# A decoder layer on one core: the values become the weight in two column tiles, and VectorE's chain is cut and put in another order

## The reference, cut to what matters

```
q, k, v = x @ Wq, x @ Wkv[:, :1024], x @ Wkv[:, 1024:]     # 16 heads of 64
sim  = q k^T / 8
G    = sigmoid(sim)
P    = min(flip(cumsum(flip(G))), 63)                       # position of key j for query i
E    = q @ pos_emb                                          # 64 table entries for each query
sim += w * E[ceil(P)] + (1 - w) * E[floor(P)]               # w = P - floor(P)
out  = softmax(sim) @ v;  result = concat(out) @ Wout + b_out
```

## Time and profile before

| | us |
|---|---|
| median of 3 runs | 2726.79 (2726.04 to 2726.97) |
| span of the profiled execution | 2722.5 |
| PE busy in the span | 2562.4 (94%) |
| DVE busy | 2256.0 (83%) |
| ACT busy | 1501.2 (55%) |
| POOL busy | 214.1 (8%) |

### The profile page before, as it was taken

One profiled execution on the slowest core, in us unless ns is written; L12 is line 12 of the kernel. 1 busy time (PEld: TensorE's weight loads), 2 busy tenths in 40 slices (PEclk: granted clock), 3 DMA queues, 4 the chain that ended last, 5 costly groups with the idle time before them and its releaser, 6 DMA issues. The chain is left out here.

```text
span 2722.5 us, 69322 instructions
## 1 busy us (share of the span) xinstructions
PE 2562.4 (94%) x18175; PEld 2259.5 (83%) x18175; DVE 2256.0 (83%) x5821; ACT 1501.2 (55%) x2487; POOL 214.1 (8%) x283
## 2 busy tenths in 40 slices
PE   6999999999999999999999999999999997999997
PEld 5888888888888888888888888888888885777776
DVE  6999999999999999999999999999999980222222
ACT  4655565556556555565555655555555552344442
POOL 0000000000000000000000000000000000111111
PEclk9999999999999999999999999999999998999998
DMA  2111111111111111111111111111110102001100
GB/s 81 35 39 35 39 35 39 35 39 35 37 35 37 33 37 33 39 35 39 35 39 35 39 35 39 35 36 37 34 28 25 45 10 74 26 31 35 35 23 8
DMA packets 126696, 97.59 MB, mean 36 GB/s; under 512 B 24078, under 2 KB 124559, under 8 KB 126672
## 3 DMA queue, kind: packets, MB, share of 16 engines
q1 hardware_dynamic: 126672, 97.29, 12.5%
HBM read 13.21 MB, written 2.10 MB: 6 GB/s over the span
## 5 line engine op out<-in xcount | busy, mean ns | idle before, releaser
L494 PE MATMUL out<-V,probsT 128*128 (+1 forms) x8192 | 959.5, 273 | 0.0
L494 PEld LDWEIGHTS out<-V,probsT 128*128 128x128 f32 x8192 | 944.5, 192 | 0.9
L361 ACT ACTIVATE probsT<-ring 128x512 f32<-128x512 f32 x1024 | 584.5, 597 | 503.4 <-PE ring L482 503.4
L482 PEld LDWEIGHTS ring<-ident,probs 128*128 128x128 f32 x4096 | 474.7, 141 | 250.3 <-issue 170.9
L482 PE MATMUL ring<-ident,probs 128*128 128x128 f32 x4096 | 580.1, 274 | 98.4 <-DVE k_lo L704 98.2
L369 ACT ACTIVATE probs<-Sc,nbias 128x1024 f32<-128x1024 f32 x512 | 543.2, 1112 | 232.7 <-DVE nbias L674 232.5
L657 DVE TENSOR_REDUCE mx<-Sc 128x1 f32<-128x1024 f32 (+1 forms) x640 | 636.3, 994 | 0.9 <-PE Sc L474 0.8
L474 PE MATMUL Sc<-k_hi,q_now 128*128 (+1 forms) x1024 | 469.5, 458 | 17.2 <-ACT probs L369 10.3
L621 DVE COPY_PREDICATED z<-mask,z 128x96 f32<-128x96 int16 (+6 forms) x896 | 422.1, 471 | 30.8
L474 PE MATMUL Sc<-k_lo,q_now 128*128 (+1 forms) x1024 | 406.6, 397 | 0.0
L297 POOL TENSOR_TENSOR prod<-frac,z 128x350 f32<-128x350 f32 x128 | 142.5, 1113 | 2085.2 <-DVE z L644 2085.2
(11 more groups left out here) (117 smaller groups left out, 2392.5 us busy)
## 6 DMA issues: line engine op xcount, KB each, us to landing
q_far<-q SPq DMA_DIRECT2D x128, 128.0 KB, 2.0
q_now<-q SPq DMA_DIRECT2D x128, 128.0 KB, 2.0
xv<-xT SPq DMA_DIRECT2D x113, 128.0 KB, 2.2
k_hi<-k_hi SPq DMA_DIRECT2D x128, 64.0 KB, 1.9
k_lo<-k_lo SPq DMA_DIRECT2D x128, 64.0 KB, 1.9
at<-attn SPq DMA_DIRECT2D x16, 512.0 KB, 3.2
q<-stage SPq DMA_DIRECT2D x120, 64.0 KB, 1.9
probs<-in_x_dram SPq DMA_DIRECT2D x4, 512.0 KB, 5.5
```

What stands on the lines that cost most here:

```text
L361: nc.scalar.activation(probsT[:, u, 4 * s:4 * s + 4, :], ring[(k + s) % 2][:, :].rearrange("p (t q) -> p t q", q=P), ACT.Copy).then_inc(sl ...
L482: last = nc.tensor.transpose(ring[(k + s) % 2][:, j * P:(j + 1) * P], probs[:, u, (4 * s + j) * P:(4 * s + j + 1) * P], ident[:, :])
L494: last = nc.tensor.matmul(out[:, 0:VW], probsT[:, u, t, :], V[:, h % 4, t, :], start=t == 0, stop=t == NT - 1)
```

## The change

1. **V as the weight.** V loses its column of ones. At the first g of each head SP copies the head's values into a tile `V_now` (512 KB, `load_values`), once `outputs` of the head before are done. In `outputs` the 64 columns of `V_now[:, t, :]` are now the weight and 128 columns of probsT stream past them. Even t go to partitions 0 to 63 of `out`, odd t to partitions 64 to 127, so there are two column tiles, each with its own sum. ACT copies both halves out (`empty_halves`), and one more matmul against a matrix of two stacked identities (`fold`) adds and transposes them into columns 128 to 191 of `out` (`turn`).
2. **The row sums** come from ACT's exponentials (`accum_out`, one sum for each half). DVE adds the two (`add_halves`) and inverts the sum from SBUF.
3. **DVE's chain** loses mask 7 and the shift by 128. The scans of the next g stand ahead of `last_shift`; `corrections` moves from the end of the body to behind the first `bank_max` of the next body; `scale(g - 1, 0)` moves from the end of body g - 1 to behind `scan_floors` in body g; and `scale(g - 1, 1)` moves behind shift 3. Semaphore `scanned` is split into `scanned` and `shifted`, and three tiles share memory with others (`flo = rnd`, `frac = cut`, `corr = prod`).

```diff
-BITS = 8
+BITS = 7
+TURN = P
...
+            def load_values(g):
+                sp.dma_start(V_now[:, :, :], V[:, (g // PAIRS) % 4, :, :]).then_inc(v_in, 16)
...
+                if head:
+                    wait_apart(sp, out_full, g * 2, waited)
+                    load_values(g)
...
+            def empty_halves(g, u):
+                act.wait_ge(out_full, g * 2 + u + 1)
+                nc.scalar.activation(halves[:, u, :], out[:, 0:P], ACT.Copy).then_inc(halves_out, 1)
...
-                    nc.scalar.activation(probs[:, u, cols], Sc[:, cols], ACT.Exp,
-                                         bias=nbias[:, u:u + 1]).then_inc(exp_done, 1)
+                    nc.scalar.activation(probs[:, u, cols], Sc[:, cols], ACT.Exp, bias=nbias[:, u:u + 1],
+                                         accum_out=sums[:, u, half:half + 1]).then_inc(exp_done, 1)
...
                 exps(g, 0)
+                if not first:
+                    empty_halves(g - 1, 1)
                 if val:
-                    if not first:
-                        act.wait_ge(out_full, g * 2)
                     values(g, base, k)
...
                 if wait_read and tiles[0] == 0:
                     pe.wait_ge(out_read, g * 2 + u)
+                if tiles[0] == 0:
+                    wait_apart(pe, v_in, g // PAIRS * 16 + 16, waited)
                 for t in tiles:
                     if t % 4 == 0:
                         pe.wait_ge(slot_out, base + k + t // 4 + 1)
-                    last = nc.tensor.matmul(out[:, 0:VW], probsT[:, u, t, :], V[:, h % 4, t, :],
-                                            start=t == 0, stop=t == NT - 1)
+                    half = t % 2 * C
+                    last = nc.tensor.matmul(out[half:half + C, 0:P], V_now[:, t, :], probsT[:, u, t, :],
+                                            start=t < 2, stop=t >= NT - 2)
...
+            def turn(g, u):
+                pe.wait_ge(halves_out, g * 2 + u + 1)
+                nc.tensor.matmul(out[:, TURN:TURN + C], halves[:, u, :], fold[:, :],
+                                 start=True, stop=True).then_inc(turned, 1)
...
                     if n < 2:
                         logits(g, 1, n + 2)
+                    if n == 1 and not first:
+                        turn(g - 1, 1)
...
+            def add_halves(g, u):
+                dve.wait_ge(exp_done, g * 4 + u * 2 + 2)
+                nc.vector.tensor_tensor(rowsum[:, u:u + 1], sums[:, u, 0:1], sums[:, u, 1:2],
+                                        ALU.add).then_inc(summed, 1)
...
                 bank_max(g, 0, 0, 0, 1, 2)
+                if not first:
+                    corrections(g)
                 add_window(g, 0)
                 if chain:
                     scan_floors(c)
+                if not first:
+                    scale(g - 1, 0)
                 window_max(g, 0, 1, 2, 4)
...
                 if chain:
-                    shift(c, 7)
+                    shift(c, 6)
                 if proj:
                     k_rest(g + PAIRS, 0)
                 if chain:
-                    shift(c, 6)
-                if chain:
                     shift(c, 5)
-                if not first:
-                    invert(g - 1, 1)
                 bank_max(g, 1, 0, 0, 1, 2)
                 if not first:
-                    scale(g - 1, 1)
+                    add_halves(g - 1, 1)
                 if chain:
                     shift(c, 4)
                 add_window(g, 1)
+                if not first:
+                    invert(g - 1, 1)
                 if chain:
                     shift(c, 3)
+                if not first:
+                    scale(g - 1, 1)
...
                     slopes(c)
-                    last_shift(c)
-                invert(g, 0)
+                add_halves(g, 0)
                 if scan:
                     scan_positions(c + 1)
-                scale(g, 0)
+                invert(g, 0)
                 if scan:
                     round_positions(c + 1)
                 if chain:
-                    corrections(c)
+                    last_shift(c)
```

More of the change, by code:

```diff
@@ L120, in attention @@
         stage = sb("stage", [P, STEP], F32R)
-        V = sb("V", [P, 4, NT, VW])
+        V = sb("V", [P, 4, NT, C])
+        V_now = sb("V_now", [P, NT, C])
+        halves = sb("halves", [P, 2, P])
+        fold = sb("fold", [P, C])
+        sums = sb("sums", [P, 2, 2])
+        rowsum = sb("rowsum", [P, 2])
         q_far = sb("q_far", [P, 2 * P], F32R)
@@ L270, in body @@
                     load_now(g + 1)
-            with sp.Fori(0, LASTV // PAIRS - 1) as h:
-                with sp.Fori(0, PAIRS) as t:
+            with sp.Fori(0, PAIRS) as g:
+                body(g)
+            weights(2)
+            with sp.Fori(1, LASTV // PAIRS - 1) as h:
+                body(h * PAIRS, head=True)
+                with sp.Fori(1, PAIRS) as t:
                     body(h * PAIRS + t)
                 weights(h + 2)
-            with sp.Fori(LASTV - PAIRS, LASTV) as g:
+            body(LASTV - PAIRS, head=True)
+            with sp.Fori(LASTV - PAIRS + 1, LASTV) as g:
                 body(g)
             weights(H - 1, values=False)
-            with sp.Fori(LASTV, LASTP) as g:
+            body(LASTV, tile=False, head=True)
+            with sp.Fori(LASTV + 1, LASTP) as g:
                 body(g, tile=False)
@@ L283, in _ @@
             load_early(sp, A, A["ctx_in"])
-            with sp.Fori(LASTP, G - 2) as g:
+            body(LASTP, late=True, proj=False, tile=False, head=True)
+            with sp.Fori(LASTP + 1, G - 2) as g:
                 body(g, late=True, proj=False, tile=False)
@@ L293, in _ @@
                            channel_multiplier=0).then_inc(consts, 1)
+            for half in range(2):
+                pool.wait_ge(consts, 2 + half)
+                nc.gpsimd.affine_select(out=fold[:, :], in_=fold[:, :], compare_op=ALU.not_equal, fill=1.0,
+                                        base=-half * C, pattern=[[-1, C]], channel_multiplier=1).then_inc(consts, 1)
             def body(c):
-                pool.wait_ge(scanned, c * CH + CH)
+                pool.wait_ge(shifted, c * CH + CH)
                 nc.gpsimd.tensor_tensor(prod[:, :, 1:W], frac[:, :, 1:W], z[:, 1, :, 1:W],
@@ L551, in _ @@
             outputs(G - 1, 1, base, 0)
+            turn(G - 1, 1)
         @block.vector
@@ L612, in masks @@
                     nc.vector.tensor_scalar(mask[:, b, :, :], dist[:, :, :], 2 << b, None,
[L613 removed]
+                                            ALU.bitwise_and).then_inc(shifted, 1)
             def shift(c, b):
[L617 to L618 removed]
+                top = b == BITS - 1
+                after(c, f"mask {b}" if top else f"shift {b + 1}")
+                if top:
                     wait_apart(dve, near_out, c * 2 + 2, waited)
@@ L683, in scale @@
                 dve.wait_ge(rsum_done, g * 2 + u + 1)
-                nc.vector.tensor_scalar(attn[:, t * 2 + u, bass.ds(h * C, C)], out[:, 0:C], rsum[:, u:u + 1],
-                                        None, ALU.mult).then_inc(out_read, 1)
+                wait_apart(dve, turned, g * 2 + u + 1, waited)
+                nc.vector.tensor_scalar(attn[:, t * 2 + u, bass.ds(h * C, C)], out[:, TURN:TURN + C],
+                                        rsum[:, u:u + 1], None, ALU.mult).then_inc(out_read, 1)
             def q_rest(s, par):
@@ L794, in _ @@
             body(G - 1, chain=False, scan=False, proj=False)
+            scale(G - 1, 0)
+            add_halves(G - 1, 1)
             invert(G - 1, 1)
```

61 lines of the change are left out of this document (37 added, 24 removed).

## The result

The changed kernel takes **2749.5 us** (median of 4 runs, 2748.2 to 2752.2) against 2726.9 for the kernel before (2726.0 to 2727.1): ratio 1.0085, interval 1.0070 to 1.0099. In every run on record the time of an execution exceeds its own span by 1.8 to 2.3 us. So only some 2 of the 4.3 us that were put around the span lie there; the rest is the spread between executions.

What follows compares the result with a forecast made beforehand. DVE's row bounds the kernel at 17.26 us a turn; the late scale's loop makes it 8.40 + 9.74 = 18.14. 111 turns at +0.88, +5 and -2 for others, give 2828 us against 2726.8; range 2750 to 2935.

Steps and rivals of the forecast that it cites:

- DVE's row decides before, PE follows: Kernel before: DVE's instructions set the turn of 17.26 us, and PE follows with 0.8 us to spare.
- From S to X: 8.40: From first scale's end (S) over PE's outputs, projection, ACT's copies, exponentials and turn to second scale's start (X): 8.40 us.
- 0.056 apart: PE's records in `outputs` start 0.056 us apart if the two column tiles overlap fully, 0.113 without overlap.
- A: Rival: column tiles don't overlap, PE's own path to the logits decides, 18.89 a turn, 2919 us; chance 0.25.
- C: Rival: weight loads not hidden, 0.168 a record in a 64-column tile, turn 20.7, some 3130 us; chance 0.02.
- DVE will stand still 1.18 us: DVE's own work between first and second scale is 7.22 of the 8.40 us, so it waits 1.18 each turn.
- From X back to S it needs 9.74: DVE's own row from the second scale's start to the next first scale's end: 16.96 - 7.22 = 9.74 us.
- Turns without projection, "-0.30": Eight turns without projection lack the loop through the copies; DVE alone decides, 0.30 us less each.
- PE idle "2 to 3 us": PE stands idle 2 to 3 us ahead of `outputs(g - 1, 1)`, released by DVE's write of `attn`.
- Rival B: The loop is shorter than read, S to X at most 7.22, so DVE decides: 127 x -0.30, 2689 us; chance 0.12.

Runs made afterwards that it cites:

- seven bits: Kernel before without mask 7 and the shift by 128, shift 6 taking its place ahead of `k_rest`, nothing else: 2656.0 us, ratio 0.9739.
- late scale: Kernel before with only `scale(g - 1, 0)` moved from between scans and rounding to behind the floors of the next body: 3035.2 us, ratio 1.1130.
- scans behind: Changed kernel with the scans of the next g back behind `last_shift`, the rest as changed: 2957.1 us, ratio 1.0845 to the kernel before.
- early scale: Changed kernel with `scale(g - 1, 0)` right behind the first maximum, ahead of corrections, window and floors: 2677.7 us, ratio 0.9819 to the kernel before.

## Why the prediction was right in direction and wrong in size

- **DVE's row decides before, PE follows:** right. PE lost 269 us of busy time and nothing came of it; seven bits on DVE alone gave 2656.
- **"From S to X: 8.40":** 8.53. PE's start 0.25 (0.27), outputs with mode changes 0.62 (0.65), projection 1.52 (1.52), copies 0.79 (0.77), exponentials with sums and the copy of the halves up to the transposes 2.81 (2.79), to the turn 1.65 (1.64), turn 0.56 (0.56). Only DVE's start behind the turn is off: 0.33 for 0.20.
- **Column tiles "0.056 apart":** 0.054, and 0.111 when one tile is used. Rivals A and C fall for the changed kernel.
- **"DVE will stand still 1.18 us":** 0.57 + 0.33 = 0.90, in the stretch forecast. The other 7.63 of the 8.53 are DVE's own row, which I had priced at 7.22; since the loop decides there, this error cost nothing. DVE waits mostly for `k_hi` in `q_rest`, and only the rest of it for the turn; I had named `turned` and `bank_full`.
- **"From X back to S it needs 9.74":** this is the step that failed; it measured 9.00. In it I priced the two scans by their distance of 1.54 to the next start in the kernel before, and moved them, at that price, to a place where POOL is idle. They measure 0.85 there: 0.69 of the 0.74. POOL's multiply, away from the scans, takes 0.94 instead of 1.11, which brings the corrections 0.17 forward; small terms of the other sign, the reciprocal and the start of the rounding above all, make 0.1. The mechanism (the loop through the late scale) was right, and so were its links; the term of DVE's row that it closes with was mis-sized. The hint stood in the trace of before: two pairs of scans of the same shape, 505 and 845 ns, the slower one beside POOL. The sum with these terms: 18.14 - 0.69 - 0.17 + 0.13 (S to X) + 0.1 = 17.51, measured 17.54.
- **Turns without projection, "-0.30":** -0.91, mostly by the same term.
- **PE idle "2 to 3 us":** 1.49. The scale ends 3.16 us into DVE's body (1028.18 to 1031.34), near the 3.3 forecast; but PE reaches those outputs only when its transposes end, 1.96 us into it (1030.14), and not at its start as before.
- **Rival B** ("DVE decides"): wrong for the change as made, but it is what the kernel becomes once the scale stands 1.1 us of work earlier. Its price of 16.96 a turn had the same error in the scans; that kernel's turn is 16.46.
- **The range** took its bounds from signals, mode changes and sums. The duration of a moved instruction was in no bound, and it was the term that moved.

The Trainium skill (SBUF — State Buffer, 🔬 SBUF: two separate sides) says that VectorE and GpSimd share a pair of ports, that a VectorE operation with two SBUF inputs and a GpSimd operation that reads SBUF exclude each other there, and that the later one is blocked for the whole instruction. The trace agrees, in direction and in size. The first scan, which came first, kept its 0.52; the multiply took 0.17 longer, with 175 columns and with two, as it would if it waited for the end of that scan; and the second scan, alone 0.50 long, ended 0.39 behind the multiply. The maximum, which reads PSUM, was not slowed. That the ports are the cause is the skill's account; the runs show the waiting and its size.

## What to carry to other kernels

Price a moved instruction by what it takes without its old neighbours and beside its new ones; the same shape elsewhere in the trace shows it. Look at the instances one by one: a mean of 845 ns stood for one of 0.52 and one of 1.20 us. Where engines run in order, an early release behind which another engine's row stands is worth more than the few hundred ns of work that pass it: moving one 0.28 us write cost or gave 70 to 310 us here. Savings on one engine don't add up once a loop over several engines is the bound; look for what waits behind each of them, and move the release before anything is made shorter.

## What the runs showed of the hardware

- Two DVE scans with both inputs in SBUF take 0.93 us while POOL is idle and 1.62 beside a multiply on POOL that starts 0.12 behind the first. The first scan isn't slowed (0.52), the second takes 1.20. The multiply takes 1.11 there and 0.94 away from them. A maximum over 1024 columns of PSUM beside the same multiply took 1.22, and 1.21 with the multiply cut short.
- Two column tiles of 64 with different weights run side by side: 0.054 us for each record of 128 columns in f32, against 0.111 in one. Their loads, 0.137 us long each, are hidden, although all tiles use the same rows. The Trainium skill (TensorE: Matmul & The Clock Gate, Part 3, The mechanism) says that a load overlaps matmuls in flight only where the row groups differ; that doesn't hold for them.
- An exponential with an accumulated sum is followed by an instruction of its own, 0.19 to 0.20 us long, of which 0.09 shows in the distance of starts.
- The granted clock fell most often in the kernels where PE's gaps are longest. With 1.49 us idle ahead of the outputs in every turn the changed kernel lost it only in the first of its 127 turns; with 1.80 (late scale) it was lost in 70 turns, down to a mean of 0.76, and with 2.58 (scans behind) in 80. But no length of gap separates the turns: with the same 2.58 some stayed at 1.00, and one late turn of the kernel before fell to 0.90 with no gap over 1.10. The kernel with the early scale lost it in ten turns, seven of them its last ones, where the gap is up to 2.16:

```profile
2084.50:2101.80 17.30, 14.28 (x126) 11.90 (x124) 15.24 (x42) 10.06 (x21) 0.94 (x1) 0.90 0.04 15
```

That the gaps are the cause is argued from this and not shown, and why only some turns of a kernel lose the clock stays open; no run was made for it.
